# First phase of a conditioned transformer block: directions ahead of the rotations, both normalisations on ScalarE, gates inside the last group, masks loaded in the setup

## The chip, the cores and the metric

One core of a Trainium2 chip runs the whole program. The metric is the time of one execution on the device in microseconds, taken as the median of several runs.

## What is computed

Two batch elements of 2048 tokens with 256 channels go through a conditioned block: a layer norm that is scaled and shifted by vectors of a condition, an attention of 8 heads of 32 dimensions with a second "geometric" attention beside it, a gated residual, a second layer norm of the same kind, and two layers of local attention with a feed-forward part. The change lies in what leads to the first attention:

```python
mod = (_silu(L0_c) @ L0_wmod).reshape(L0_c.shape[0], 6, 1, -1)
sa, ca, ga, sb, cb, gb = ...                   # planes 0 to 5 of mod
ga = (2 * (ga >= 0) - 1) * jnp.maximum(jnp.abs(ga), 0.25)     # gb the same
h = _layernorm(x, axis=-1) * (1 + ca) + sa
# inside the attention, x is this h
xn = (x - mu) * jax.lax.rsqrt(var + 1e-05) * ln_g + ln_b
q, k, v = xn @ Wq.T, xn @ Wk.T, xn @ Wv.T      # in heads
q, k = _apply_rope(q, cos, sin), _apply_rope(k, cos, sin)
attn = softmax(where(causal, q @ k.T * scale, -inf))
qp, kp = einsum('bhtd,hd->bht', q[..., :3], head_dirs), ...   # the same of k
geo_attn = softmax(where(causal, qp[..., :, None] * kp[..., None, :], -inf))
```

A row's maximum of the geometric scores needs only the running maximum and minimum of kp up to that token. The kernel computes those as "directions".

## The kernel before

The program is a row of blocks, each with its own instruction stream per engine; at the end of a block the engines wait for each other. `setup_phase` computes the condition's six planes `S.mod` and the first normalisation of the first group. `qkv_phase`, here "the first phase", runs over 8 groups (`GROUPS`) of 512 tokens (four tiles of 128), four groups for each batch element. `attention_phase` then runs over 16 pairs of batch element and head, and the projection and the two layers follow. Each engine works its instructions in the order of the code and waits on semaphores; nothing is reordered.

Within a group n of the first phase, with lines of the kernel before:

- VectorE takes `statistics(n+1)` of the tokens in `xin` (mean and variance, `var` at L410). Then it makes four rotations (u = 0 to 3: two halves of q, two of k), each three instructions: `rot_c` L443, `rot_s` L444, their sum `qk` L449. A rotation waits for the product in `qk_ps`, which has two buffers, and releases it after L444. Between the rotations stand pieces of the next group: after u = 0 `modulated` (the normalised `xhat`, L418, times 1 + ca, L421), and behind it `directions(n-1)` (L462 to L469, on 8 partitions); after u = 1 `shifted` (`h_now`, L426, and its statistics, `var` at L429); after u = 2 `normed` (`hn`, L435). `low_part` (L453) subtracts the rounded part `hi` from `qk`. The group ends with two of these.
- GpSimd loads the tokens (L307) and raises the variance plus epsilon to the power -1/2: `rstd` at L309 for the first normalisation and at L302 for the second. The load for group n+2 is issued behind the second power of group n+1.
- ScalarE copies: `hi` (L328) after each rotation, `values` from `v_ps` (L331) after the third and fourth, the two rows of dots (L340), the transposed tokens `xnt` with the norm's gain and bias (L319), and `h_now` to its keeping place (L321).
- TensorE multiplies for the four rotations (L367), for the values (L377), makes the dots of q with the directions (L387), transposes `hn` of the next group (L356), and makes the dots of k (L387). The last waits for the copy of the dots of q, since both use one bank.
- SyncE sends a group's parts of q and k (eight stores, L279), then the directions' row of the group before (`send_geo`, L270), then the two rows of dots (L284, L285). The directions of a group wait until the row of the group before has landed, because they write the same tile `run`.

After the last group VectorE makes the `gates` (planes 2 and 5 of `S.mod`, L475 to L481) and the last directions, and SyncE sends their row as its last instruction of the phase.

In the attention's block GpSimd first issues three loads of masks (L913 to L915), which TensorE's first product (L971, L973) needs. SyncE loads the dots (L870), then the second head's operands (L516), then the geo rows (L788); TensorE transposes the dots (L1028) after three products. VectorE clears its tiles (L1151 to L1156) and takes chunk maxima (L1091).

## Time and profile before

| what | before |
|---|---|
| median of 3 runs | 2773.08 us (2772.15 to 2776.82) |
| profiled execution | 2774.7 us, span 2773.0 |
| TensorE / VectorE / ScalarE / GpSimd busy | 92% / 79% / 56% / 20% of the span |
| first phase, from VectorE's first instruction in its block to the first memset of the next | 23.00 to 263.25 us |
| attention's first product | 270.98 us |

The page's line of busy tenths gives a rough map; the first four of its forty slices are the setup and the first phase. The stretches, the timelines of single engines and the lines of single instructions give the rest. Times in a timeline are counted from the start of the span.

### The profile page before, as it was taken

To read this page: it belongs to the slowest core of one execution; us is meant where nothing else is said; L and a number is where in the kernel's file an instruction comes from. 1 tells how busy PE (TensorE), PEld (TensorE's weight loads), DVE (VectorE), ACT (ScalarE), POOL (GpSimd) and SP (SyncE) were. 2 spreads that over 40 slices of the span, in tenths; PEclk is the share of its full clock that TensorE was granted. 3 is DMA by queue.
4 is the path that set the end of the run, shared out by engine and by line. 5 is a ranking of instruction groups with operands and counts; after the bars stand their busy time and mean duration, and the time that the engine had idled before them with its cause. 6 is when DMAs were issued, how large, how long until landed. Compare 5 with 4: busy or idle time off the path is not lost. (4 is left out here: it accounts for less than half of the span.)

```text
span 2773.0 us, 45283 instructions
## 1 busy us (share of the span) xinstructions
PE 2563.4 (92%) x14104; PEld 1546.1 (56%) x14104; DVE 2187.4 (79%) x4633; ACT 1563.8 (56%) x3449; POOL 549.9 (20%) x389
## 2 busy tenths in 40 slices
PE   7886999999999999996999999989989999997998
PEld 3333433333333333334677777678867777775777
DVE  5877999999999999985788888656558888885665
ACT  1221566667766666762666666634336666664442
POOL 1100011111111100106333333200023333331000
PEclk9998899999999999998999999999989999999999
DMA  3234355445455445453100000030020000001121
GB/s 127 78 115 115 85 139 141 120 110 132 112 139 140 121 108 128 119 180 110 59 16 20 17 15 21 16 131 20 7 60 10 9 8 9 8 13 47 46 67 39
DMA packets 124741, 204.95 MB, mean 74 GB/s; under 512 B 22736, under 2 KB 71952, under 8 KB 121280
## 3 DMA queue, kind: packets, MB, share of 16 engines
q1 hardware_dynamic: 111856, 170.39, 22.1%
q0 software_dynamic: 8688, 21.27, 2.7%
q10 hardware_dynamic: 4080, 11.86, 1.2%
q8 instruction: 58, 0.95, 0.1%
q14 instruction: 59, 0.48, 0.1%
HBM read 125.44 MB, written 54.13 MB: 65 GB/s over the span
## 5 line engine op out<-in xcount | busy, mean ns | idle before, releaser
L1059 ACT ACTIVATE probs<-st_ps 128x512 f32<-128x512 f32 (+3 forms) x640 | 339.9, 531 | 294.1 <-PE st_ps L988 163.7
L1112 DVE SCALAR_TENSOR_TENSOR geo_x<-geo_rows,kp_t 128x512 f32<-128x512 f32 (+3 forms) x640 | 438.1, 708 | 4.5 <-ACT probs L1061 4.5
L1091 DVE TENSOR_REDUCE chunk_max<-a_ps 128x1 f32<-128x512 f32 (+3 forms) x640 | 359.1, 603 | 41.1 <-PE a_ps L971 27.0
L1061 ACT ACTIVATE probs<-geo_x 128x512 f32<-128x512 f32 (+3 forms) x640 | 361.4, 565 | 13.9 <-DVE geo_x L1118 13.8
L1391 PE MATMUL local_in_ps<-w_local,local_ht 128*128 128x512 f32 x1152 | 324.4, 419 | 9.5 <-ACT local_sq L1533 5.4
L1552 ACT ACTIVATE local_probs<-local_s_ps,local_bias,local_inv 128x256 f32<-128x256 f32 x512 | 283.2, 564 | 14.0 <-DVE local_bias L1647 14.0
L1830 PE MATMUL ff_ag_ps<-ff_ht_parts,w 128*128 128x512 f32 (+1 forms) x1056 | 257.6, 402 | 17.0 <-DVE ff_gate L1939 8.9
L1003 PE MATMUL o_ps<-probs,vx_first 128*33 128x512 f32 (+3 forms) x1280 | 270.6, 544 | 0.0
L1003 PE MATMUL o_ps<-probs,vx_ 128*33 128x512 f32 (+3 forms) x1280 | 270.3, 544 | 0.0
L1559 ACT ACTIVATE local_pt<-local_pt_ps 128x512 f32<-128x512 f32 x256 | 152.5, 596 | 207.7 <-PE local_pt_ps L1449 199.6
L1643 DVE TENSOR_REDUCE local_top<-local_s_ps 128x4 f32<-128x1024 f32 x128 | 156.8, 1225 | 121.2 <-PE local_s_ps L1435 121.2
L1391 PEld LDWEIGHTS local_in_ps<-w_local,local_ht 128*128 128x128 f32 x1152 | 209.1, 194 | 58.7 <-issue 18.8
L1830 PEld LDWEIGHTS ff_ag_ps<-ff_ht_parts,w 128*128 128x128 f32 (+1 forms) x1056 | 198.8, 191 | 71.0 <-DVE ff_gate L1939 16.6
L1654 DVE TENSOR_SCALAR local_probs<-local_probs,local_rden 128x256 f32<-128x256 f32 x512 | 223.0, 477 | 9.0
L1722 POOL TENSOR_TENSOR local_inv<-local_norm,half 128x16 f32<-128x16 f32 x64 | 186.5, 2915 | 175.3 <-DVE local_norm L1632 108.1
L1843 PE MATMUL ff_y_ps<-ff_w,ff_act_t 128*128 128x256 f32 x1152 | 148.6, 285 | 14.5 <-DVE ff_act_t L1945 13.9
L1459 PE MATMUL local_o_ps<-local_pt,local_v_ring 128*64 128x128 f32 x2048 | 154.6, 282 | 3.3 <-ACT local_pt L1559 3.1
L1449 PE MATMUL local_pt_ps<-ident,local_probs 128*128 128x128 f32 x1024 | 149.9, 279 | 6.5 <-DVE local_probs L1654 1.4
L367 PE MATMUL qk_ps<-xnt,w_qkv 128*128 128x512 f32 x256 | 128.2, 659 | 26.3 <-DVE rot_s L444 25.4
L1843 PEld LDWEIGHTS ff_y_ps<-ff_w,ff_act_t 128*128 128x128 f32 x1152 | 139.5, 190 | 21.2 <-DVE ff_act_t L1945 21.0
L971 PE MATMUL a_ps<-k_first,q_first 96*128 96x512 f32 (+2 forms) x320 | 120.8, 451 | 33.0 <-DMA later<-in_mask_t 16.9
L1435 PE MATMUL local_s_ps<-local_k_t,local_q_t 64*128 64x256 f32 x1024 | 146.1, 404 | 0.6 <-ACT local_q_t L1546 0.6
(193 smaller groups left out, 4155.0 us busy)
## 6 DMA issues: line engine op xcount, KB each, us to landing
geo_rows<-geo SPq DMA_DIRECT2D x64, 512.0 KB, 7.6
piece_lo<-in_pieces POOLq DMA_DIRECT2D x15, 768.0 KB, 5.7
weight_parts<-piece_hi SPq DMA_DIRECT2D x15, 768.0 KB, 3.4
weight_parts<-piece_lo SPq DMA_DIRECT2D x15, 768.0 KB, 6.0
raw<-out_t SPq DMA_DIRECT2D x128, 64.0 KB
shares_in<-shares SPq DMA_DIRECT2D x64, 128.0 KB, 4.7
q_first<-q_parts SPq DMA_DIRECT2D x24, 256.0 KB, 4.2
k_first<-k_parts SPq DMA_DIRECT2D x24, 256.0 KB, 6.3
```

Source lines behind the costliest of these rows:

```text
L1003: ins = pe.matmul(o_ps[kind * HALF:kind * HALF + VW, g % 2, off:GTOK], vx[s][:, j, :], probs[:, i % PSLOTS, kind, off:GTOK], start=j == 0, ...
L1059: act.activation(probs[:, s % PSLOTS, 0, off:GTOK], st_ps[:, (b * NB + s) % STBANKS, off:GTOK], ACT.Exp).then_inc(q["st_used"], 1)
L1061: act.activation(probs[:, s % PSLOTS, 1, off:GTOK], geo_x[:, s % GSLOTS, off:GTOK], ACT.Exp).then_inc(q["probs_ready"], 1)
L1091: dve.reduce_max(chunk_max[:, it, c:c + 1], a_ps[:, n % ABANKS, 0:width], AX.X).then_inc(q["a_used"], 1)
L1112: ins = dve.scalar_tensor_tensor(out[:, off:GTOK], geo[:, 1, at], kp_t[:, j, ds(b, 1)].rearrange("p o -> p o"), geo[:, 0, at], ALU.add, AL ...
L1391: last = pe.matmul(in_ps[:, j, :], ht[:, p, a, k, :], w[:, b, k, j * INNER:(j + 1) * INNER], start=i == 0, stop=i == len(steps) - 1)
L1552: last = act.activation(probs[:, hd, :], s_ps[:, a, x % 2 * 2 * P:(x % 2 + 1) * 2 * P], ACT.Exp, bias=bias[:, hd:hd + 1], scale=inv[:, p, ...
L1643: dve.tensor_reduce(top[:, hs].rearrange("p (x a) -> p x a", x=2), s_ps[:, :, :].rearrange("p a (x n) -> p x a n", x=2), AX.X, ALU.max).th ...
L1654: last = dve.tensor_scalar(probs[:, hd, :], probs[:, hd, :], rden[:, hd:hd + 1], None, ALU.mult)
L1722: pool.tensor_tensor(inv[:, p, :], norm2[:, :], S.half[:, :], ALU.pow).then_inc(q["inv_done"], 1)
L1830: last = pe.matmul(ag_ps[0:rows, x % 2, half, :], w1[:, a, k, c0:c0 + rows], ht_parts[:, b, k, :], start=i == 0, stop=i == len(steps) - 1)
L1843: last = pe.matmul(y_ps[:, t, :], act_t[:, a, x, t * P:(t + 1) * P], w2[:, b, x, :], start=(x, i) == (0, 0), stop=x == HC - 1 and i == len ...
```

## The change

Five things are changed.

1. `directions(n-1)` stands at the start of group n, behind `statistics(n+1)` and ahead of the first rotation. SyncE sends the row of group n-1 at the start of its turn n, ahead of the eight stores. The last row is sent as the first instruction of SyncE in the attention's block; the tiles for it lie on the other side of the memory.
2. Both normalisations go from VectorE to ScalarE, as `rstd * x + offset` with `offset = -mean * rstd`. VectorE makes the negated mean (`centre`), GpSimd multiplies. ScalarE does the first (`normalised`) at the start of a group and the second (`normed`) ahead of its fourth `hi`.
3. ScalarE keeps `h_now` (`keep`) at the end of its group and no longer between `xnt` and the second copy of dots.
4. `gates` is cut in two, for planes 2 and 5, and runs in the last group behind its first and second rotation; the addition on plane 4 stands ahead of the last `low_part`.
5. The three masks are loaded by GpSimd in the setup, into tiles that stay. Two tiles of the attention (`raw_0`, `raw_1`) change places in memory.

```diff
@@ Shared @@
+        self.mask_n, self.mask_t = sb("mask_n", [P, P], BF16), sb("mask_t", [P, P], BF16)
+        self.later = sb("later", [P, P])
@@ setup_phase, gpsimd @@
                 pool.dma_start(S.ident_bf[:, :], io["ident"]).then_inc(rounded, 16)
+                pool.dma_start(S.mask_n[:, :], io["mask_n"]).then_inc(S.attention_masks_in, 16)
+                pool.dma_start(S.mask_t[:, :], io["mask_t"]).then_inc(S.attention_masks_in, 16)
+                pool.dma_start(S.later[:, :], io["mask_t"]).then_inc(S.attention_masks_in, 16)
@@ new helper @@
+def send_geo(sp, S, n):
+
+    heads, tokens = group_place(n)
+    sp.wait_ge(S.first["geo_ready"], n + 1 + START)
+    sp.dma_start(S.geo[heads, 1, tokens], S.last_geo[:, :]).then_inc(S.first["geo_out"], 16)
@@ qkv_phase, sync @@
                 def send(n, geo_too):
+                    if geo_too:
+                        send_geo(sp, S, n - 1)
                     sp.wait_ge(q["hi_done"], 4 * n + 4 + START)
                     sp.wait_ge(q["lo_done"], 4 * n + 4 + START)
...
-                    if geo_too:
-                        send_geo(n - 1)
                     sp.wait_ge(q["dot_used"], 2 * n + 2 + START)
...
-                send_geo(GROUPS - 1)
@@ gpsimd @@
                 def second_scale(n):
                     pool.wait_ge(q["var2"], n + 1 + START)
                     pool.tensor_tensor(rstd[:, 1, :], var[:, 1, :], S.half[:, 0:GT], ALU.pow).then_inc(q["rstd2"], 1)
+                    pool.wait_ge(q["rstd2"], 2 * n + 1 + START)
+                    pool.tensor_tensor(offset[:, 1, :], centre[:, 1, :], rstd[:, 1, :], ALU.mult).then_inc(q["rstd2"], 1)
...
                     pool.tensor_tensor(rstd[:, 0, :], var[:, 0, :], S.half[:, 0:GT], ALU.pow).then_inc(q["rstd1"], 1)
+                    pool.wait_ge(q["rstd1"], 2 * n + 1 + START)
+                    pool.tensor_tensor(offset[:, 0, :], centre[:, 0, :], rstd[:, 0, :], ALU.mult).then_inc(q["rstd1"], 1)
@@ scalar @@
+                def keep(n):
                     act.activation(S.h1[:, ds(n * GT, GT), :], h_now[:, :, :], ACT.Copy).then_inc(q["h_kept"], 1)
 
+                def normalised(n):
+                    act.wait_ge(q["rstd1"], 2 * n + 2 + START)
+                    for t in range(GT):
+                        last = act.activation(xhat[:, t, :], xin[:, t, :], ACT.Identity, bias=offset[:, 0, t:t + 1], scale=rstd[:, 0, t:t + 1])
+                    last.then_inc(q["x_used"], 1)
+
+                def normed(n):
+                    act.wait_ge(q["rstd2"], 2 * n + 2 + START)
+                    act.wait_ge(q["xt_ready"], CC * n + START)
+                    for t in range(GT):
+                        last = act.activation(hn[:, t, :], h_now[:, t, :], ACT.Identity, bias=offset[:, 1, t:t + 1], scale=rstd[:, 1, t:t + 1])
+                    last.then_inc(q["hn_ready"], 1)
+
                 def group(n, more):
+                    if more:
+                        normalised(n + 1)
                     for u in range(4):
+                        if u == 3 and more:
+                            normed(n + 1)
                         act.wait_ge(q["rope_done"], 4 * n + u + 1 + START)
...
                         act.activation(dots_sb[:, u, :], dot_ps[:, :], ACT.Copy).then_inc(q["dot_used"], 1)
+                    if more:
+                        keep(n + 1)
@@ vector @@
+                    dve.tensor_scalar(centre[:, 0, :], mv[:, :, 0], -1.0, None, ALU.mult)
                     dve.tensor_scalar(var[:, 0, :], mv[:, :, 1], EPS, None, ALU.add).then_inc(q["var1"], 1)
...
-                        dve.wait_ge(q["rstd1"], n + 1 + START)
-                        for t in range(GT):
-                            last = dve.tensor_scalar(xhat[:, t, :], xin[:, t, :], mv[:, t, 0:1], rstd[:, 0, t:t + 1], ALU.subtract, ALU.mult)
-                        last.then_inc(q["x_used"], 1)
                         dve.wait_ge(q["x_used"], n + 1 + START)
...
                     if more:
                         statistics(n + 1)
-                    for u, piece in enumerate((modulated, shifted, normed, None)):
+                    if begun:
+                        directions(n - 1, first)
+                    for u, piece in enumerate((modulated, shifted, None, None)):
                         rotate(n, u)
                         if u:
                             low_part(n, u - 1)
                         if more and piece:
                             piece(n + 1)
-                        if u == 0 and begun:
-                            directions(n - 1, first)
+                        if not more and u in (0, 1):
+                            gates((2, 5)[u])
+                    if not more:
+                        dve.tensor_scalar(S.mod[:, 4, :, :], S.mod[:, 4, :, :], 1.0, None, ALU.add)
                     low_part(n, 3)
...
-                gates()
                 directions(GROUPS - 1, False)
@@ attention_phase @@
+            send_geo(sp, S, GROUPS - 1)
             sp.dma_start(dots[:, 1, :], S.dots).then_inc(q["dots_in"], 16)
...
-            pool.dma_start(mask_n[:, :], io["mask_n"]).then_inc(masks_in, 16)
-            pool.dma_start(mask_t[:, :], io["mask_t"]).then_inc(masks_in, 16)
-            pool.dma_start(later[:, :], io["mask_t"]).then_inc(masks_in, 16)
```

The rows below are the instructions of an engine in the order of the built program, with the shape of what each writes; x4 means four in a row. First VectorE at the start of group 1, before:

```order
L410 TENSOR_SCALAR var<-mv 128x4
L443 SCALAR_TENSOR_TENSOR rot_c<-qk_ps,cos_t 128x512
L444 SCALAR_TENSOR_TENSOR rot_s<-qk_ps,sin_t 128x512
L449 TENSOR_TENSOR qk<-rot_c,rot_s 128x512
L418 TENSOR_SCALAR xhat<-xin,mv,rstd 128x256 x4
L421 TENSOR_TENSOR xhat<-xhat,mod 128x1024
L462 SCALAR_TENSOR_TENSOR run<-dots_sb 8x512
L463 SCALAR_TENSOR_TENSOR run<-dots_sb 8x512
L465 COPY carry<-run 8x1 x2
L467 SCALAR_TENSOR_TENSOR run<-dots_sb,run 8x512
L468 SCALAR_TENSOR_TENSOR run<-dots_sb,run 8x512
L469 SCALAR_TENSOR_TENSOR run<-run 8x512
```

The same place in the changed program:

```order
L446 TENSOR_SCALAR centre<-mv 128x4
L447 TENSOR_SCALAR var<-mv 128x4
L488 SCALAR_TENSOR_TENSOR run<-dots_sb 8x512
L489 SCALAR_TENSOR_TENSOR run<-dots_sb 8x512
L491 COPY carry<-run 8x1 x2
L493 SCALAR_TENSOR_TENSOR run<-dots_sb,run 8x512
L494 SCALAR_TENSOR_TENSOR run<-dots_sb,run 8x512
L495 SCALAR_TENSOR_TENSOR run<-run 8x512
L469 SCALAR_TENSOR_TENSOR rot_c<-qk_ps,cos_t 128x512
L470 SCALAR_TENSOR_TENSOR rot_s<-qk_ps,sin_t 128x512
L475 TENSOR_TENSOR qk<-rot_c,rot_s 128x512
L454 TENSOR_TENSOR xhat<-xhat,mod 128x1024
```

The directions have moved ahead of the first rotation, the four instructions that normalise `xhat` are gone, and a `centre` has come in. Next ScalarE in its loop, from the values behind the third rotation to those behind the fourth; REGISTER_ALU and ISA are small instructions that set up the next wait or address. Before:

```order
L331 ACTIVATE values<-v_ps 128x512
L325 REGISTER_ALU
L328 ACTIVATE hi<-qk 128x512
L330 REGISTER_ALU
L331 ISA
L331 ACTIVATE values<-v_ps 128x512
```

and changed:

```order
L363 ACTIVATE values<-v_ps 128x512
L346 REGISTER_ALU
L348 ACTIVATE hn<-h_now,offset,rstd 128x256 x4
L357 REGISTER_ALU
L360 ACTIVATE hi<-qk 128x512
L362 REGISTER_ALU
L363 ISA
L363 ACTIVATE values<-v_ps 128x512
```

The four instructions for `hn` now stand in ScalarE's queue between the values of the third rotation and the `hi` of the fourth. Last GpSimd from the end of the first phase to the attention's first instructions, before:

```order
L260 UNCONDITIONAL_BRANCH
L901 UNCONDITIONAL_BRANCH
L913 DMA mask_n<-in_mask_n 128x128
L914 DMA mask_t<-in_mask_t 128x128
L915 DMA later<-in_mask_t 128x128
L946 MEMSET k_first 2x2048
```

and changed:

```order
L278 UNCONDITIONAL_BRANCH
L929 UNCONDITIONAL_BRANCH
L971 MEMSET k_first 2x2048
L971 MEMSET k_ 2x2048
L933 COPY vx_first<-values 128x16x32
```

The three loads have gone from here to the setup.

## Rows read from the trace of the kernel before

**Rows 1.** Stretches: us; busy (x instructions) of PE, PEld, DVE, ACT, POOL; PEclk, DMA, GB/s.

```profile
0.00:22.00 22.00, 12.46 (x24) 5.27 (x24) 5.63 (x21) 2.80 (x4) 2.05 (x7) 1.00 0.69 255
...
115.00:144.00 29.00, 24.16 (x66) 11.13 (x66) 23.29 (x53) 7.05 (x12) 2.78 (x3) 0.94 0.27 92
```

**Rows 2.** Timeline, VectorE, group 3: start us, us, what [idle before <-releaser].

```profile
120.75 0.69 DVE L443 SCALAR_TENSOR_TENSOR rot_c<-qk_ps,cos_t 128x512 f32<-128x512 f32 x1 [4.61 <-PE qk_ps L367]
...
122.78 1.38 DVE L418 TENSOR_SCALAR xhat<-xin,mv,rstd 128x256 f32<-128x256 f32 x4
...
125.86 1.27 DVE L462 TENSOR_TENSOR_SCAN run<-dots_sb,carry 8x512 f32<-8x512 f32 x1 [0.26 <-DVE xhat L421]
...
130.50 0.67 DVE L443 SCALAR_TENSOR_TENSOR rot_c<-qk_ps,cos_t 128x512 f32<-128x512 f32 x1
...
138.13 0.68 DVE L453 TENSOR_TENSOR lo<-qk,hi 128x512 fp32r<-128x512 f32 x1
...
149.48 0.69 DVE L443 SCALAR_TENSOR_TENSOR rot_c<-qk_ps,cos_t 128x512 f32<-128x512 f32 x1 [4.12 <-PE qk_ps L367]
```

**Rows 3.** Timeline, TensorE: ends of groups 0, 3 and 6, the slow product.

```profile
57.87 1.88 PE L387 MATMUL v_ps<-qk,dirs 128*8 128x512 f32 x4 [1.31 <-ACT values L331]
...
131.82 5.24 PE L367 MATMUL qk_ps<-xnt,w_qkv 128*128 128x512 f32 x8 [4.43 <-DVE rot_s L444]
...
143.75 1.88 PE L387 MATMUL v_ps<-qk,dirs 128*8 128x512 f32 x4 [0.41 <-issue]
145.56 4.99 PE L367 MATMUL qk_ps<-xnt,w_qkv 128*128 128x512 f32 x11
...
228.97 1.88 PE L387 MATMUL v_ps<-qk,dirs 128*8 128x512 f32 x4 [0.35 <-issue]
```

**Rows 4.** Timeline, ScalarE, end of group 3.

```profile
142.06 0.64 ACT L328 ACTIVATE hi<-qk 128x512 fp32r<-128x512 f32 x1 [2.55 <-DVE qk L449]
...
143.08 0.57 ACT L340 ACTIVATE dots_sb<-v_ps 8x512 f32<-8x512 f32 x1
...
144.88 1.04 ACT L321 ACTIVATE x<-h_now 128x1024 f32 x1
145.83 0.57 ACT L340 ACTIVATE dots_sb<-v_ps 8x512 f32<-8x512 f32 x1
```

**Rows 5.** Timeline, ScalarE, projection phase, and GpSimd's offset by line.

```profile
1257.34 2.09 ACT L578 ACTIVATE normed<-x,offset,rstd 128x256 f32<-128x256 f32 x4 [7.66 <-POOL offset L595]
...
L595 POOL TENSOR_TENSOR offset<-centre,rstd 128x4 f32<-128x4 f32 x8 | 1.6, 202 | 0.6
```

**Rows 6.** One line, the token load L307: time from issue to landing; its issue in group 3.

```profile
137.34 0.79 POOL L307 DMA_DIRECT2D xin<-in_x  x1
...
DMA to landing us min/median/max: 4.2/4.3/4.6
```

**Rows 7.** The line L657 and its longest instance: ns min/median/max, then timeline.

```profile
L657 DVE TENSOR_SCALAR centre<-mv x8: 170/170/986, 1245.8 to 1285.8; 128x4 f32<-128x4 f32 x8
...
1253.96 0.99 DVE L657 TENSOR_SCALAR centre<-mv 128x4 f32<-128x4 f32 x1
```

**Rows 8.** Timeline, end of the first phase: gates, geo row, last directions, next phase.

```profile
250.03 0.42 DVE L478 TENSOR_SCALAR sgn<-mod 128x512 f32<-128x512 f32 x1
...
254.37 0.60 SPq L270 DMA_DIRECT2D geo<-run  x1
...
257.60 1.27 DVE L462 TENSOR_TENSOR_SCAN run<-dots_sb,carry 8x512 f32<-8x512 f32 x1 [3.11 <-DMA geo<-run]
...
263.25 0.11 DVE L1151 MEMSET chunk_max<- 128x64 f32 x1 [0.94 <-PEq L260]
```

**Rows 9.** Timeline, start of the attention: load of the dots, first product, transposes.

```profile
263.16 0.32 SPq L870 DMA_DIRECT2D geo_rows<-dots  x1
...
270.98 0.48 PE L971 MATMUL a_ps<-k_first,q_first 96*128 96x128 f32 x1 [16.94 <-DMA later<-in_mask_t]
...
272.53 1.89 PE L1028 MATMUL st_ps<-ident,geo_rows 16*128 16x16 f32 x16
```

More of the change, by code:

```diff
@@ L244, in qkv_phase @@
         sgn, mag = sb("sgn", [P, B, C]), sb("mag", [P, B, C])
-        run = [sb(f"run{k}", [H, GTOK]) for k in range(2)]
-        carry = sb("carry", [H, 2])
+        dots_sb = sb("dots_sb", [H, 2, GTOK], side="right")
+        run = [sb(f"run{k}", [H, GTOK], side="right") for k in range(2)]
+        carry = sb("carry", [H, 2], side="right")
+        centre, offset = sb("centre", [P, 2, GT]), sb("offset1", [P, 2, GT])
+        S.last_geo = run[0]
         h_now = sb("h_now", [P, GT, C])
@@ L263, in _ @@
             def _(sp):
-                def place(n):
-                    return ds(n // GPB * H, H), ds(n % GPB * GTOK, GTOK)
-                def send_geo(n):
-                    heads, tokens = place(n)
-                    sp.wait_ge(q["geo_ready"], n + 1 + START)
-                    sp.dma_start(S.geo[heads, 1, tokens], run[0][:, :]).then_inc(q["geo_out"], 16)
                 def send(n, geo_too):
+                    if geo_too:
+                        send_geo(sp, S, n - 1)
                     sp.wait_ge(q["hi_done"], 4 * n + 4 + START)
@@ L428, in shifted @@
                     c.link(ln_stats(dve, c, stats, mv, carrier[:, :], lambda t: [h_now[:, t, :]]))
+                    dve.tensor_scalar(centre[:, 1, :], mv[:, :, 0], -1.0, None, ALU.mult)
                     dve.tensor_scalar(var[:, 1, :], mv[:, :, 1], EPS, None, ALU.add).then_inc(q["var2"], 1)
-                def normed(n):
-                    dve.wait_ge(q["rstd2"], n + 1 + START)
-                    dve.wait_ge(q["xt_ready"], CC * n + START)
-                    for t in range(GT):
-                        last = dve.tensor_scalar(hn[:, t, :], h_now[:, t, :],
-                                                 mv[:, t, 0:1], rstd[:, 1, t:t + 1], ALU.subtract, ALU.mult)
-                    last.then_inc(q["hn_ready"], 1)
                 def rotate(n, u):
@@ L683, in __init__ @@
         sb, _, _ = allocators(nc, ctx, ctx)
-        self.out_t = sb("out_t", [P, 2, GTOK], side="right")
-        self.raw = [sb(f"raw_{s}", [P, 2, GTOK], side="right") for s in range(2)]
+        raw_odd = sb("raw_1", [P, 2, GTOK], side="right")
         self.shares = sb("shares_in", [P, 2, GTOK], side="right")
         self.sums = sb("sums_in", [P, T * 2 // P], side="right")
+        self.out_t = sb("out_t", [P, 2, GTOK], side="right")
+        self.raw = [sb("raw_0", [P, 2, GTOK], side="right"), raw_odd]
         self.summed = sb("summed", [P, GTOK], side="right")
@@ L741, in attention_phase @@
     probs = sb("probs", [P, PSLOTS, 2, GTOK])
[L742 to L743 removed]
+    mask_n, mask_t, later = S.mask_n, S.mask_t, S.later
     share, out_t, raw, shares, sums, summed = ahead.share, ahead.out_t, ahead.raw, ahead.shares, ahead.sums, ahead.summed
```

31 lines of the change are left out of this document (15 added, 16 removed).

## Prediction

> **What bounds the kernel now.** The table of stretches says where to look. A group of 512 tokens in the first phase takes 29 us, and TensorE is busy for 24.2, VectorE for 23.3, ScalarE for 7.1 and GpSimd for 2.8 of it [rows 1]. Nobody is saturated, so the period is a loop of waits and I read it from the timelines of the engines. VectorE stands idle 4.61 us at a group's start, until TensorE has the first product of queries (L443) [rows 2]. TensorE in its turn starts the last product of the group 4.43 us late, because VectorE had not emptied the buffer: it was busy with 1.59 us of normalising xhat (L418) and 4.64 us of directions (L462 to L469) [rows 2, 3]. So two engines wait for each other once in a group. The loop begins at TensorE's last directions product of a group (L387), which I call S: 57.87 for group 0 and 228.97 for group 6, so six periods take 171.1 us, 28.52 each [rows 3].
>
> At S, ScalarE has just worked through a short queue: hi and values (1.02 us from 142.06), then the copy of the first dots, after which S starts at 143.75, 1.69 us behind hi [rows 3, 4].
>
> **The change, a steady group.** I walk once round the new loop from S.
> 1. TensorE's product ends and ScalarE copies it (L340). Before, the copy started 2.08 us after S, right behind the keeping copy of h (L321, ends 145.92); that now comes later, and the product itself (1.88) ends at 145.63, so I take 1.95 for its start. The copy takes 0.57, with a little for the signal 2.55 us from S to the first directions pass [rows 3, 4].
> 2. The directions now stand before the first rotation: 4.64 us [rows 2]. They need no product of this group, so they fill what was the wait. The product for the rotation is there at S+5.73 (before: S at 143.75, the wait at L443 over at 149.48 [rows 2, 3]), and the directions end at S+7.2, so VectorE no longer waits there.
> 3. From the first rotation to the end of the third VectorE took 120.75 to 138.13, 17.38 us [rows 2]. Away go the normalisation, 1.59, the directions, 4.64, and the pause of 0.26 ahead of them; a `centre` of about 0.08 comes in. That leaves 10.97.
> 4. ScalarE then does hi and values, 1.02, the four normalisations of hn, and the 1.69 to the next S. The four stand ahead of the last hi in its queue, and behind them the whole way to S waits. The same form runs in the later projection phase: four take 2.09 us, and the small `offset` on GpSimd 0.20 [rows 5]. Together 4.8. Its scale is ready early enough: a power takes 1.0 us on GpSimd (2.78 busy in a group, less 0.79 for the load's issue, halved [rows 1, 6]) and the offset 0.20, and both run while VectorE does the third rotation.
>
> The sum is 2.55 + 4.64 + 10.97 + 4.8 + 0.1 for signals = 23.05 us. I look at what else could be late. TensorE: its own work in a group is 24.2 us with eight matmuls at the slower clock; at the clock of the others (0.454 us each, 4.99 for 11) the eight cost 3.6 instead of 5.24 [rows 1, 3], so 22.5. That is close beneath. Token loads: GpSimd issues one right after the second scale, and it lands 4.2 to 4.6 us after that [rows 6]; before, the issue (137.34) came 6.84 us behind the second rotation's start (130.50), now that rotation starts at S+10.5 and a centre and an offset stand ahead of the issue, so S+17.9; plus 4.3 it is S+22.2, while VectorE asks for it at S+22.7. Hidden, by half a microsecond. ScalarE's first normalisation (another 2.09) starts at about S+3.5 and is asked for at S+9.2; hidden.
>
> Here a rule of the Trainium skill speaks against the move. "ScalarE: Activation LUTs" (Rules for kernel authors) sends adds and multiplies to VectorE and gives about 0.3 us plus 0.83 ns per element for an ACTIVATE. That is an estimate of 0.51 us for 256 elements and the trace agrees, with 0.52 (a quarter of 2.09) [rows 5]. The four steps cost more than on VectorE, 2.09 for its 1.29 to 1.59; if both engines stood on the path all the time the move would lose 0.7 us twice in a group. Only the second is on the path here.
>
> GpSimd's power of the first scale now runs beside the first pass of the directions. What that costs no group of before shows, since VectorE was idle then. The nearest row is in the projection phase: a `centre` that began while GpSimd added two tensors took 0.99 us, where the median of eight is 0.17 [rows 7]. Bounds: nothing, or 0.7 us (the time for which power and offset would still run when the pass wants to start). I take 0.3 since only part of the span overlaps: 23.4 us a group. "GPSIMD Engine Reference" (Specifications) says that GpSimd shares its SBUF interface with VectorE, with contention where VectorE has two SBUF inputs, as these passes have; by that rule alone it would be the 0.7, 2.4 us more in six groups.
>
> Six periods: 6 x (28.52 - 23.4) = **30.7 us saved**.
>
> **Start and group 0.** The normalisation of hn, four instructions of VectorE like those at L418 (1.38), becomes 2.09 on ScalarE behind an offset of 0.20, so everything begins 0.9 us later [rows 2, 5]. In group 0 TensorE runs through; its S waited 1.31 us for ScalarE [rows 3], and that wait goes, because VectorE is done some 2.7 us sooner. Together -0.2, which I count as 0. The three mask loads now stand in the setup, where TensorE waits for its first weights. They are 128 KB, half a microsecond at the 255 GB/s of the setup [rows 1]; between 0 and 0.5, and I take **0.3 lost**.
>
> **Last group and the boundary.** Before: from S of group 6 (228.97) to the first memset of the attention (263.25), 34.3 us [rows 3, 8]. In it the gates ran after the group's products, from 250.03 for 4.46 us, and the last directions then waited another 3.11 us until the geo row, which was queued behind eight stores, had landed [rows 8]. Now: directions end S+7.2; four rotations of 1.93 with two subtractions of 0.6 (8.9) and two gates of 2.23 between them make S+20.6; the last two subtractions and the 0.35 on plane 4 make S+22.2. The last directions run S+24.9 to S+29.5 (1.69 and 2.55 behind the last rotation, 4.64 long) and no longer wait for a transfer. SyncE sends eight stores (4.5) and two rows of dots from S+26.8, the last issued at S+27.4; a row like it landed 3.2 us after its issue (254.37 to 257.60) [rows 8], so the phase ends at about S+30.6 and the memset comes at S+31.1. **3.2 us saved.** The gates are not hidden where they stand; they cost the same 4.46 us ahead of the last products that they cost behind them before, and what is won is the wait.
>
> **Start of the attention.** TensorE's first product waited for the third mask until 270.98, 7.7 us after VectorE's first memset [rows 8, 9]. With masks in place it can run at once. The next thing late is the load of the dots, issued at 263.16 as SyncE's first; it now stands behind the last geo row (0.3). If it lands 3.2 us after its issue like the small row above, it is there at 266.65 on the clock of before; the transposes that need it (L1028) ran at 272.53 [rows 8, 9]. So 5.9 are saved and not 7.7. The loads that follow, for the second head and of the geo rows, then begin closer to each other and can crowd. Between 0 and 2 us; I take 0.6. **5.3 us saved.** Behind this the attention's engines follow each other, and I find no fixed point in it for which they would wait.
>
> **Sum:** 30.7 - 0.3 + 3.2 + 5.3 = **38.9 us**. The profiled execution took 2774.7 us (span 2773.0), so 2735.8; against the median of 2773.08, 1.6 lower, it is **2734.2 us**.
>
> **The rivals.**
> *The loop is longer than I walk it.* If the scans take the whole 0.7, ScalarE's four instructions do not overlap the wait for the third rotation, and the loop's register work adds to each step, a group takes 24.4: 6 us less saved, 2740. For it: the group from 120.75 to 149.48 took 28.73, 0.2 more than the mean [rows 2].
>
> *It is shorter,* 22.5, the bound by TensorE: 5.4 more, 2728.8. It needs ScalarE to be no part of the loop, against which its queue speaks.
>
> *The masks don't free the start.* Something else would hold TensorE's first product for the same time, such as the second head's load. Then 2739.5. The row names only the mask as what it waited for [rows 9].
>
> *The first phase gains, and the attention gives it back* by waiting for something set by the transfers, up to 30 us: 2745 to 2765. Nothing in the rows shows it.
>
> *Slower.* The token load gets onto the path. Directions could then start at the load's landing plus 2.3 us of statistics, and the period is 17.65 us plus the time to landing. With 4.3 that is 22, below the 23.4. It decides the period from 5.8 us on, and eats the whole gain (39 us, or 6.5 us a group) from 12.3 us to landing; at 15 the time is 2790. The seven landings of before lie within 4.2 to 4.6 [rows 6], and the stores that could crowd it still come behind it.
>
> *The change does not do what it says* in the clock: the product that ran slow after 4.43 us of waiting stays slow. TensorE's clock in that stretch was 0.94 of full on average [rows 1]; it would then be 24.2 a group, 2739. Its waits fall to about 1 us, so I count this with the longer loop.
>
> **How the numbers follow.** My forecast, with its own range of 2730 to 2738: 0.64. Longer loop 0.14, shorter 0.10, masks 0.06, gain given back 0.03, slower 0.03. The range 2727 to 2743 takes in the first four but for the ends of the shorter and longer loop. A difference of 0.2% (5.5 us) can be told from none: faster by more than that 0.96, same 0.01, slower 0.03.
>
> **What would show it.** The page of the changed kernel should show rotations' wait at the group's start gone; S to S at 23 to 24 us; the directions starting 2.5 us behind S with GpSimd's power beside them; normalisations of 0.52 us on ScalarE ending about when the fourth rotation does; VectorE's first memset of the attention near 229, its first chunk maximum within 3 us of that. Wrong would be a wait of VectorE for the token load, or a first product of the attention that still waits for a transfer.

## Result and the profile after

| | before | changed |
|---|---|---|
| median of 4 runs each, same chip | 2774.06 us (2772.15 to 2776.82) | 2732.91 us (2727.59 to 2735.83) |
| profiled execution, span | 2774.7, 2773.0 | 2730.8, 2729.1 |

The ratio is 0.985, 95% interval 0.983 to 0.9868: 41 us, or 1.5%, faster. The forecast was 2734.2 us.

A group first. The stretch of the changed kernel from 80 to 103 us (columns as in [rows 1]):

```profile
80.00:103.00 23.00, 22.23 (x64) 10.45 (x64) 21.05 (x47) 10.63 (x20) 3.81 (x5) 1.00 0.34 118
```

TensorE is now busy for 22.2 of 23 us and its clock is granted in full, where it had 24.2 of 29 at 0.94 [rows 1]. From S of group 0 to S of group 6 it takes 137.56 us, 22.93 a group, where it was 28.52 [rows 3]. Both ends, and two S in between, in TensorE's timeline (start, duration, what, idle before and its releaser):

```profile
57.45 1.88 PE L423 MATMUL v_ps<-qk,dirs 128*8 128x512 f32 x4
...
99.79 1.88 PE L423 MATMUL v_ps<-qk,dirs_q 128*8 128x512 f32 x4 [0.37 <-ACT values L363]
101.84 1.09 PE L392 MATMUL tp<-ident,hn 128*128 128x128 f32 x8 [0.17 <-ACT hn L348]
103.27 1.88 PE L423 MATMUL v_ps<-qk,dirs 128*8 128x512 f32 x4 [0.34 <-issue]
...
126.38 1.88 PE L423 MATMUL v_ps<-qk,dirs 128*8 128x512 f32 x4 [0.34 <-issue]
...
195.01 1.88 PE L423 MATMUL v_ps<-qk,dirs 128*8 128x512 f32 x4 [0.34 <-issue]
```

TensorE's only waits in a group are the three of 0.37, 0.17 and 0.34 us. The 4.43 us of waiting for `rot_s`, and the product at the slower clock behind it, are gone [rows 3].

VectorE from S (103.27) on:

```profile
105.90 1.27 DVE L488 TENSOR_TENSOR_SCAN run<-dots_sb,carry 8x512 f32<-8x512 f32 x1 [0.77 <-ACT dots_sb L372]
107.10 1.25 DVE L489 TENSOR_TENSOR_SCAN run<-dots_sb,carry 8x512 f32<-8x512 f32 x1
...
110.54 0.67 DVE L469 SCALAR_TENSOR_TENSOR rot_c<-qk_ps,cos_t 128x512 f32<-128x512 f32 x1
...
121.62 0.69 DVE L479 TENSOR_TENSOR lo<-qk,hi 128x512 fp32r<-128x512 f32 x1
...
125.36 0.69 DVE L479 TENSOR_TENSOR lo<-qk,hi 128x512 fp32r<-128x512 f32 x1 [0.54 <-ACT hi L360]
126.23 1.41 DVE L232 BATCH_NORM_STATS2 stats<-xin 128x6 f32<-128x256 f32 x4 [0.17 <-DMA xin<-in_x]
```

The first rotation (110.54) has no wait any more; it had 4.61 [rows 2]. ScalarE and GpSimd beside it:

```profile
105.22 1.03 POOL L320 TENSOR_TENSOR rstd<-var,half 128x4 f32<-128x4 f32 x1 [5.68 <-DVE var L447]
106.33 0.84 POOL L322 TENSOR_TENSOR offset<-centre,rstd 128x4 f32<-128x4 f32 x1
...
107.20 2.07 ACT L341 ACTIVATE xhat<-xin,offset,rstd 128x256 f32<-128x256 f32 x4 [0.49 <-POOL offset L322]
...
121.73 0.63 ACT L360 ACTIVATE hi<-qk 128x512 fp32r<-128x512 f32 x1 [5.16 <-DVE qk L475]
122.27 0.58 ACT L363 ACTIVATE values<-v_ps 128x512 f32 x1
122.75 2.06 ACT L348 ACTIVATE hn<-h_now,offset,rstd 128x256 f32<-128x256 f32 x4
124.71 0.62 ACT L360 ACTIVATE hi<-qk 128x512 fp32r<-128x512 f32 x1
```

The end of the phase and the start of the attention, VectorE, SyncE's queue and TensorE:

```profile
219.91 1.27 DVE L488 TENSOR_TENSOR_SCAN run<-dots_sb,carry 8x512 f32<-8x512 f32 x1 [2.71 <-ACT dots_sb L372]
...
222.43 0.60 SPq L295 DMA_DIRECT2D dots<-dots_sb  x1
...
225.68 0.11 DVE L1176 MEMSET chunk_max<- 128x64 f32 x1 [1.06 <-PEq L278]
225.79 0.44 PE L996 MATMUL a_ps<-k_first,q_first 96*128 96x128 f32 x1 [6.54 <-PEq L278]
...
228.88 1.88 PE L1053 MATMUL st_ps<-ident,geo_rows 16*128 16x16 f32 x16 [1.51 <-DMA geo_rows<-dots]
```

The first product runs as soon as the block begins, no longer 7.7 us later, and the transposes follow the memset by 3.20 us instead of 9.28 [rows 8, 9].

Where 43.65 us went, up to VectorE's first `geo_x` of the attention (288.75 us before, 245.10 now):

| stretch | before | changed | saved | forecast |
|---|---|---|---|---|
| start to S of group 0 | 57.87 | 57.45 | 0.42 | -0.3 |
| six groups | 171.10 | 137.56 | 33.54 | 30.7 |
| S of group 6 to the memset | 34.28 | 30.67 | 3.61 | 3.2 |
| memset to first `geo_x` | 25.50 | 19.42 | 6.08 | 5.3 |

From the first `geo_x` to the end of the span both take the same, 2484.25 and 2484.00 us. In executions of the changed kernel that part varies, from 2480.4 to 2484.2 in three of them, and over all kernels here from 2477.0 to 2490.0, with no code changed in it. So medians tell a microsecond or two badly, and below the marks of the profiled executions decide. One of the four executions of e1 below took 5096.46 us, nearly twice the others, and nothing on record says why; it is left out of e1's median.

### The profile page after: what moved, and what is told of

Its sections match the earlier page's. It is cut to its first block and busy times, and to the rows that moved or that the text cites. A ratio compares the mean times of both kernels' runs of the same rounds, so it can differ in the third digit from the quotient of the medians.

```text
span 2729.1 us, 45326 instructions
## 1 busy us (share of the span) xinstructions
PE 2551.3 (93%) x14104; PEld 1541.0 (56%) x14104; DVE 2171.9 (80%) x4588; ACT 1589.6 (58%) x3509; POOL 554.8 (20%) x404
## 3 DMA queue, kind: packets, MB, share of 16 engines
q1 hardware_dynamic: 111856, 170.39, 22.2%
## 5 line engine op out<-in xcount | busy, mean ns | idle before, releaser
L1742 POOL TENSOR_TENSOR local_qk_nat<-local_rot_c,local_rot_s 128x512 f32<-128x512 f32 x64 | 82.8, 1294 | 303.4 <-PE local_pt_ps L1438 302.2
L1475 PEld LDWEIGHTS local_pt_ps<-ident,local_probs 128*128 128x128 f32 x1024 | 113.9, 141 | 51.3 <-issue 23.0
```

What stands on the lines that cost most here:

```text
L1475: last = pe.transpose(pt_ps[:, x % 2, (2 * a + s) * P:(2 * a + s + 1) * P], probs[:, 2 * x + a, s * P:(s + 1) * P], S.ident[:, :])
```

## The experiments

All on the changed kernel unless it is said otherwise, with the kernel before run beside each. "Period" is the mean of six from S to S. Ratios are to the kernel before.

| run | period | S6 to memset | memset to transposes | first `geo_x` | median, ratio [interval] |
|---|---|---|---|---|---|
| before | 28.52 | 34.28 | 9.28 | 288.75 | |
| changed | 22.93 | 30.67 | 3.20 | 245.10 | 2732.91, 0.985 |
| a0 | 22.93 | 30.63 | 3.28 | 245.22 | 2732.36, 0.9849 [0.9831, 0.9867] |
| a1 | 22.93 | 30.64 | 3.45 | 246.22 | 2731.48, 0.9835 [0.9821, 0.9849] |
| e1 masks late | 22.93 | 30.71 | 9.42 | 250.08 | 2734.72, 0.985 [0.9828, 0.9872] |
| e2 gates last | 22.93 | 29.46 | 3.17 | 243.18 | 2727.95, 0.9834 [0.9815, 0.9853] |
| e3 directions back | 26.34 | 34.67 | 3.26 | 269.62 | 2760.51, 0.9945 [0.9927, 0.9963] |
| e4 directions alone | 25.37 | 30.03 | 9.18 | 264.94 | 2751.78, 0.9915 [0.989, 0.994] |
| e5 hn on VectorE | 23.87 | 30.70 | 3.39 | 250.54 | 2738.34, 0.9864 [0.9839, 0.9889] |
| e8 keep ahead | 23.87 | 30.73 | 3.27 | 250.64 | 2740.05, 0.9875 [0.9856, 0.9894] |
| e9 one tile on VectorE | 22.90 | 30.70 | 3.09 | 243.85 | 2732.42, 0.9849 [0.9824, 0.9873] |
| e10 gates and dots | 22.92 | 29.46 | 3.12 | 243.10 | 2725.55, 0.9825 [0.9808, 0.9842] |
| e11 fewer products | 22.92 | 30.61 | 3.14 | 244.46 | 2730.72, 0.9832 [0.9811, 0.9853] |
| e12 half scale | 22.39 | 30.77 | 3.39 | 241.02 | 2727.09, 0.9819 [0.9801, 0.9836] |

**The changed kernel again**, twice.

> The changed kernel itself, on this chip, as the reference for the others: about 41 us below the kernel before (2733), S to S (from one group's last directions product to the next) 22.9 us, from S of group 6 to VectorE's first memset of the attention 30.7 us, from that memset to the transposes of the dots 3.2 us.

> The changed kernel once more, on the same chip as the three others, so that the smaller differences have their own reference. Period 22.93, S of group 6 to the first memset 30.6, memset to transposes 3.2, first geo_x at 245.1; median 2729 to 2736.

The period and the stretch from S of group 6 to the memset repeat within 0.05 us, and the stretch from the memset to the transposes within 0.25. The start does not: S of group 0 came at 57.45, 57.55 and 58.38.

**The directions' place.** e4 does this part alone, on the kernel before (only the last row stays in the first phase, where it was):

```diff
                 def send(n, geo_too):
+                    if geo_too:
+                        send_geo(n - 1)
...
-                    if geo_too:
-                        send_geo(n - 1)
...
+                    if begun:
+                        directions(n - 1, first)
                     for u, piece in enumerate((modulated, shifted, normed, None)):
...
-                        if u == 0 and begun:
-                            directions(n - 1, first)
```

> Kernel before with one part of the change: directions at the group's start and their row sent ahead of the eight stores. Normalisations stay on VectorE, gates and masks stay where they were. S to S = 2.65 + 4.64 + 16.3 + 1.7 = 25.3 us instead of 28.5, so 19 us in six periods, and 2 to 3 us at the last directions, which no longer wait for the row: 22 us faster than before. Rival: the wait for the first product just moves elsewhere (VectorE is 23 of 28.5 us busy and the normalisations keep it the bound): under 8 us.

and e3 puts them back behind the first rotation in the changed kernel, with SyncE's early row kept:

```diff
-                    if begun:
-                        directions(n - 1, first)
...
+                        if u == 0 and begun:
+                            directions(n - 1, first)
```

> Changed kernel with the directions back behind the first rotation and the product with 1 + ca; all else as changed. If the directions filled VectorE's wait for the first product, the wait comes back and the 4.64 us come on top: S to S = 5.7 + 10.9 + 4.6 + 4.8 = 26.1 us instead of 22.9, the run 19 to 22 us slower than the changed kernel. Rival: the gain was the normalisations', and the place of the directions is indifferent: under 5 us.

Alone the move is worth 3.15 us a group, and 23.8 us at the first `geo_x`. At the boundary it saves 4.25 us (30.03 for 34.28), more than the 3.61 of the whole change; the runs on the gates below say why. Undone it costs 3.41 a group. The wait it was meant to fill is back in e3, VectorE at the first rotation:

```profile
115.53 0.69 DVE L469 SCALAR_TENSOR_TENSOR rot_c<-qk_ps,cos_t 128x512 f32<-128x512 f32 x1 [4.18 <-PE qk_ps L403]
```

So more than half of the 5.59 a group is the order of VectorE's work. The rest comes with the two normalisations and the place of `keep`; the first normalisation was not moved back in any run. First `geo_x` of e3 comes 24.5 us later than in the changed kernel, more than the 19 to 22 expected of the run: 20.5 are the six groups (26.34 for 22.93), and 4.0 are lost at the boundary, where the last group has its directions on the path in the same way.

**The normalisation of hn on ScalarE, and what stands in its queue.** e5 gives hn back to VectorE as before:

```diff
-                        if u == 3 and more:
-                            normed(n + 1)
...
-                    for u, piece in enumerate((modulated, shifted, None, None)):
+                    for u, piece in enumerate((modulated, shifted, normed, None)):
```

> Changed kernel with the second normalisation (hn) back on VectorE, the first still on ScalarE. If VectorE's and ScalarE's parts of the loop follow each other, VectorE gets 1.29 us more ahead of the fourth rotation, ScalarE's 2.07 before the fourth hi go, and the 0.6 of the fourth subtraction's wait too: S to S = 2.55 + 4.64 + 10.97 + 0.6 + 1.29 + 1.93 + 1.7 = 23.7 us, 4 to 5 us slower than the changed kernel. Start of group 0 0.9 us earlier. Rival, by the plain cost of the two engines (2.07 against 1.38): the run is faster, by up to 4 us.

e8 leaves it on ScalarE and puts `keep` ahead of the last `hi`:

```diff
                         if u == 3 and more:
                             normed(n + 1)
+                            keep(n + 1)
...
-                    if more:
-                        keep(n + 1)
```

> Changed kernel with the keeping copy of h (1.04 us on ScalarE, 0.95 with its overlap) moved between the normalisation of hn and the fourth hi. If ScalarE's queue there is part of the loop, a group gets 0.95 us longer (23.9) and the run 5.7 us slower. Rival: TensorE is the bound (22.0 busy plus 0.9 of waits in 22.9) and ScalarE has slack; then a group gets at most 0.5 us longer.

Both cost 0.94 us a group, where 0.8 and 0.95 were expected. For e8 that is the keeping copy nearly in full, which ScalarE now does on the way to S; TensorE's row shows the wait (the line number differs by one):

```profile
104.89 1.88 PE L422 MATMUL v_ps<-qk,dirs 128*8 128x512 f32 x4 [1.28 <-ACT values L364]
```

1.28 where the changed kernel has 0.34. What stands ahead of the last `hi` in ScalarE's queue is on the path, and what stands behind it is free. For e5, ScalarE's four instructions take 2.06 and VectorE's 1.48 for the same work, and the move to the slower engine still gains, since they no longer delay the fourth rotation. A rival that prices the move by the two durations alone has the wrong sign. "ScalarE: Activation LUTs" (Rules for kernel authors) in the Trainium skill gives such multiplies to VectorE; its price for one agreed with the row, but the queues decided, not the price.

**Who bounds the new loop?** With TensorE at 22.2 of 23 us I had two readings: TensorE itself, or the ring through VectorE's rotations and ScalarE's queue. e9 was the first try, one of hn's four tiles back on VectorE, between the third rotation and the fourth:

```diff
-                    for t in range(GT):
+                    for t in range(GT - 1):
                         last = act.activation(hn[:, t, :], h_now[:, t, :], ACT.Identity, ...)
...
-                    for u, piece in enumerate((modulated, shifted, None, None)):
+                    for u, piece in enumerate((modulated, shifted, last_tile, None)):
```

> Changed kernel with one of the four tiles of hn normalised by VectorE, between the third and the fourth rotation, the other three by ScalarE. If ScalarE's queue is what the fourth hi waits for by about 0.5 us, a group gets 0.2 to 0.35 us shorter and the run 1 to 2 us faster than the changed kernel. Rival: TensorE is the bound; then no difference in S to S (below 0.1).

No gain (22.90): my theory missed it, and the rival, a bound by TensorE, seemed to hold. But e9's own trace speaks for the ring:

```profile
100.56 0.63 ACT L360 ACTIVATE hi<-qk 128x512 fp32r<-128x512 f32 x1 [0.37 <-DVE qk L482]
...
102.24 1.88 PE L423 MATMUL v_ps<-qk,dirs 128*8 128x512 f32 x4 [0.56 <-ACT values L363]
```

ScalarE saves 0.49 us (1.57 for 2.06), but its last `hi` now waits 0.37 for VectorE's fourth rotation, which comes 0.43 later, counted from S (19.38 for 18.95). TensorE then waits 0.56 ahead of S, where it was 0.34. The work had only changed hands within the ring. To be sure, each side was shortened on its own. e11 takes work from TensorE. It leaves two of the eight products of the values out, so it computes something else and only its time is used:

```diff
-                            for k in range(CC):
+                            for k in range(t, CC):
                                 last = pe.matmul(v_ps[:, u, t * C:(t + 1) * C], ...,
-                                                 start=k == 0, stop=k == CC - 1)
+                                                 start=k == t, stop=k == CC - 1)
```

> The changed kernel with two of the eight products of the values left out in each group (for half the tokens only one half of the channels is summed), 0.9 us less of TensorE's work in each group. Theory A, TensorE bounds the period (22.2 of 22.93 busy): the period falls by 0.9 to 22.0. Theory B, the loop through VectorE's rotations and ScalarE's queue bounds it, and TensorE only follows closely: the product of the dots waits for ScalarE's copy of the values (0.37 in the changed kernel) and will wait 0.9 longer, some 1.3 us, and the period stays at 22.9 (22.85 to 22.95). After the run in which a tile of hn was moved to VectorE without a gain I hold B for likelier, 0.7.

and e12 takes work from VectorE, by leaving half of `xhat` unscaled:

```diff
-                    c.link(dve.tensor_tensor(xhat[:, :, :], xhat[:, :, :], mod(n, 1), ALU.mult))
+                    part = xhat[:, 0:GT // 2, :]
+                    c.link(dve.tensor_tensor(part, part, ..., ALU.mult))
```

> The changed kernel with VectorE multiplying only two of the four tiles of xhat by 1 + ca, 0.61 us less of VectorE's work between the first and the second rotation; the other two tiles stay unscaled. Theory B (the loop through VectorE): everything from the second rotation on comes 0.6 sooner, until TensorE stops it: its busy time is 22.07 to 22.2 and it has a gap of 0.34 ahead of the last product, so the period falls to 22.4 (22.3 to 22.5). Theory A (TensorE bounds): the period stays at 22.9, and VectorE waits 0.6 more.

The stretch from 80 to 103 us and TensorE's product of the dots in e11, then in e12:

```profile
80.00:103.00 23.00, 21.26 (x61) 9.69 (x60) 20.89 (x47) 10.64 (x20) 3.78 (x5) 1.00 0.35 118
...
99.30 1.88 PE L423 MATMUL v_ps<-qk,dirs_q 128*8 128x512 f32 x4 [1.23 <-ACT values L363]
```

```profile
80.00:103.00 23.00, 22.60 (x66) 10.59 (x66) 20.93 (x52) 10.76 (x20) 3.78 (x5) 1.00 0.37 124
...
97.69 1.88 PE L423 MATMUL v_ps<-qk,dirs_q 128*8 128x512 f32 x4
```

e11 has 0.9 us less of TensorE's work in a group and the same period to 0.01; the work turns into a longer wait for ScalarE's copy, 1.23 for 0.37. e12 has 0.54 us less on VectorE (0.68 where it was 1.22), and the period falls by the same 0.54. The ring through VectorE and ScalarE bounds the loop and TensorE follows closely: in e12 its waits for `values` and `hn` are gone, and only the 0.34 ahead of the last product is left. Those two waits, 0.37 and 0.17, are the 0.54 that the period fell by. So at 22.39 the group is TensorE's own work and that 0.34; whether anything more could be gained from VectorE was not tried.

**The masks.** e1 moves the three loads back to the attention's block:

```diff
-                pool.dma_start(S.mask_n[:, :], io["mask_n"]).then_inc(S.attention_masks_in, 16)
...
+            pool.dma_start(S.mask_n[:, :], io["mask_n"]).then_inc(S.attention_masks_in, 16)
```

> Changed kernel with the three mask loads back in the attention's block. If the masks held the attention's first product and nothing else would, the first product comes about 5 us after VectorE's first memset again (in the kernel before 7.7), the transposes behind it, and the run is 5 to 6 us slower than the changed kernel; the setup gives back 0.3. Rival: the second head's load or the dots' load hold the start anyway; then the difference is under 1 us.

TensorE's first product in e1, the wait it replaces in the changed kernel:

```profile
232.31 0.47 PE L996 MATMUL a_ps<-k_first,q_first 96*128 96x128 f32 x1 [14.34 <-DMA later<-in_mask_t]
```

It comes 7.9 us behind the memset (about 5 were expected), the transposes 9.42, and first `geo_x` 6.2 later counted from the memset. As the forecast had it, the masks were worth about 6 and not 7.7, since the load of the dots comes next. By the median e1 is only 2.4 us above a0 on the same chip, where 5 to 6 were expected; its first `geo_x` comes 4.9 us later than a0's (6.2, less 1.4 by which its S of group 0 came earlier), and the other 2.5 lie within the spread of the part behind. What the loads cost in the setup can't be told: S of group 0 came at 56.18 without them, and at 56.3 to 58.4 in eleven executions with them.

**The gates.** e2 puts both behind the last group's products, where they stood before:

```diff
-                        if not more and u in (0, 1):
-                            gates((2, 5)[u])
...
+                        gates(2)
+                        gates(5)
```

> Changed kernel with the two gates and the addition on plane 4 behind the last subtraction of the last group. Theory A (my walk of the last group: VectorE sets its end, each gate costs its 2.23 us): the last directions start 3 to 4.5 us earlier and the run is 3 us faster. Theory B (in the last group TensorE's chain of products ends last: 14 us of products from 196.8, values 3.6, dots 1.8, ScalarE's copy, dots 1.8): the gates stand in shadow, the last directions start only 0.6 us earlier, and the run is 0.5 to 1 us faster.

VectorE in e2, from the end of the gates to the first memset of the attention:

```profile
217.76 0.69 DVE L506 SCALAR_TENSOR_TENSOR mod<-sgn,mag 128x512 f32<-128x512 f32 x1
218.72 1.27 DVE L488 TENSOR_TENSOR_SCAN run<-dots_sb,carry 8x512 f32<-8x512 f32 x1 [0.27 <-ACT dots_sb L372]
...
223.80 0.11 DVE L1176 MEMSET chunk_max<- 128x64 f32 x1 [0.37 <-PEq L278]
```

This is the expectation's theory B. Behind the products the gates fill the wait for the last dots: 0.27 is left of the 2.71 that the changed kernel has. The scan starts 0.52 sooner, counted from S of group 6 (24.38 for 24.90), and the memset another 0.7 sooner, since its wait falls from 1.06 to 0.37. Ahead of the last products the gates hold up the last `lo`, with it the eight stores and the row of dots behind them (issued at 222.43 in the changed kernel, 219.00 in e2). The memset follows that issue by 3.25 us in the changed kernel, 3.29 in e1 and 3.27 in e9, and by 4.80 in e2. From this I take it that in the first three the row's landing ends the phase, and in e2 VectorE does; the view itself names only TensorE's branch. So this part of the change is a loss, of 1.2 us, and not neutral.

**The best of them.** e10 is e2 with one thing more, the load of the dots ahead of the last geo row:

```diff
-            send_geo(sp, S, GROUPS - 1)
             sp.dma_start(dots[:, 1, :], S.dots).then_inc(q["dots_in"], 16)
+            send_geo(sp, S, GROUPS - 1)
```

> The changed kernel with both gates behind the last group's products, as in the run that put the gates last, and with the load of the dots issued ahead of the last geo row. Nobody needs the geo row before the geo rows are loaded, while the transposes wait for the dots. Theory: the gates give 1.2 us between the last S and the first memset, as they did alone (30.63 to 29.46), and the transposes follow the memset by 3.2 - 0.3 = 2.9 us, since an issue takes about 0.3 on SyncE's queue. First geo_x 1.5 to 2.3 us earlier than in the changed kernel (245.1 to 245.2): 243.2 at the latest. Rival: the geo row then lands later and the load of the geo rows behind it waits for it, and the transposes gain 0.3 that first geo_x doesn't show. Median near 2729, where the changed kernel has 2732.

```profile
223.69 0.32 SPq L897 DMA_DIRECT2D geo_rows<-dots  x1
...
223.78 0.11 DVE L1176 MEMSET chunk_max<- 128x64 f32 x1 [0.37 <-PEq L278]
...
226.90 1.88 PE L1053 MATMUL st_ps<-ident,geo_rows 16*128 16x16 f32 x16 [1.42 <-DMA geo_rows<-dots]
```

The load leaves 0.35 us earlier and takes 3.21 to be used, where it took 2.93 in e2 (224.04 to 226.97), so only 0.05 of the 0.3 arrives; that expectation missed. From S of group 6 to first `geo_x` e10 takes 48.8 us, and the changed kernel 50.1 and 50.3. Its median on the same chip, 2725.55, is the lowest of all and 5.9 below a1's, but the intervals overlap, and by the marks only 1.3 to 1.5 of that are its own, nearly all of it e2's (48.84).

## Why the prediction was right, and where it was off

**The walk, step by step**, from S of group 2 (103.27) to the next. Step 1, S to the first directions pass: 2.63 measured, 2.55 forecast. Step 2, the directions: 4.64, as forecast. Step 3, first rotation to the end of the third: 110.54 to 121.62, 11.08 for 10.97. Step 4, to the next S: 4.76 for 4.8 and 0.1 of signals. Together 23.11, where the sum without contention was 23.05. The four rows of hn take 2.06, its scale and offset are in time, and the rest of ScalarE's queue is as walked.

**The contention term was wrong.** I added 0.3 us a group for GpSimd's power beside the first pass. The pass takes 1.27 us, as in [rows 2], and the power 1.03. What is stretched is GpSimd's own `offset`: 0.20 alone, and 0.84 beside the first scan. It ends when that scan ends (106.33 + 0.84 and 105.90 + 1.27 are both 107.17), and so it is, within 0.01 us, in all six groups that have a scan there. The power, which already runs when the scan begins, keeps its 1.03 and doesn't hold the scan up. The seven instances in the changed kernel, and in e3, where the scans come later (ns min/median/max, then the places):

```profile
L322 POOL TENSOR_TENSOR offset<-centre,rstd x7: 198/757/996, 37.7 to 175.3; 128x4 f32<-128x4 f32 x7
```

```profile
L322 POOL TENSOR_TENSOR offset<-centre,rstd x7: 201/201/203, 37.7 to 192.3; 128x4 f32<-128x4 f32 x7
```

ScalarE's normalisation of xhat then starts 0.4 late (S+3.93), ends at 109.27, and is asked for at 112.55, so nothing comes of it. "GPSIMD Engine Reference" (Specifications) in the Trainium skill names contention where VectorE has two SBUF inputs. There is some, but its price fell on GpSimd and not on VectorE, and the estimate of 0.7 from that rule was too high.

**The mean is not the looped group.** I walked a group in the middle. The six periods of the changed kernel are 22.71, 23.11, 23.11, 23.10, 22.71 and 22.82. The three long ones are groups 2 to 4, which are VectorE's loop; the others are written out. The mean lies 0.18 below the looped group. With the 0.3 above this makes the gap from 23.4 to 22.93 but for roundings: six times 0.47 are 2.8 of the 4.75 us that the sum fell short.

**The rest of the shortfall.** Start and group 0: 0.42 saved instead of 0.3 lost. The setup's end moved by 0.31 in this pair (VectorE's first copy of `mod`: 21.00 for 20.69), and group 0 took 0.7 less than I gave it. That the first matches the forecast is luck: the same copy came at 20.34 to 21.83 in eleven executions with the loads there, and at 20.13, 20.33 and 20.69 in three without. S of group 0 varies by 2 us, so this term is not proved either way. The wait of 1.31 us ahead of S of group 0 did go, as forecast. Boundary: 3.61 for 3.2, with the row of dots issued at S+27.42 (forecast S+27.4) and the memset at S+30.67 (S+31.1). Start of the attention: 6.08 for 5.3; the transposes came 3.20 behind the memset, as the landing of the small row told, and of the 0.6 for crowding nothing was seen.

**The gates** were the step that was wrong in its reason. The prediction held that they cost their 4.46 us at either place and that the gain was the wait for the geo row. The gain is that wait, but at the old place the gates would now cost about nothing (e2), because VectorE waits there for TensorE and ScalarE in any case: behind both gates 0.27 us of that wait are still left.

**The rivals.** The token load stayed off the path, but not out of VectorE's waits. It landed in 4.2 to 4.4 us, as forecast, but behind S of group 2 it was issued at S+18.58 (121.85) and not at S+17.9, and VectorE waited 0.17 us for it at 126.23; behind those statistics it waits 0.68 for the dots anyway, so nothing is lost. In group 0 it waited much longer, and had another 4.46 us to wait for TensorE's first product behind it:

```profile
34.41 1.41 DVE L232 BATCH_NORM_STATS2 stats<-xin 128x6 f32<-128x256 f32 x4 [6.42 <-DMA xin<-in_x]
```

So a wait for the token load, named as a sign of being wrong, did appear, and was harmless. The longer loop did not come; the shorter one (22.5, bound by TensorE) is where e12 arrives, with 22.39. The clock is 1.00 in the loop, and the slow product is gone with the wait ahead of it. In e3 both are back; in e4 there is a shorter wait and no slow product:

```profile
125.01 5.40 PE L403 MATMUL qk_ps<-xnt,w_qkv 128*128 128x512 f32 x8 [2.83 <-DVE rot_s L470]
```

```profile
121.70 3.70 PE L367 MATMUL qk_ps<-xnt,w_qkv 128*128 128x512 f32 x8 [1.27 <-DVE rot_s L444]
```

The granted clock of that group was 0.94 in e3 and 1.00 in e4.

One sign named ahead was missed: the first chunk maximum was to come within 3 us of the attention's first memset, and came 3.61 behind it (229.29), right at the end of the long copy described in the last section.

The saving at the marks was 43.65 us against 38.9. That the time came within 1.3 us of the forecast owes something to the part behind, whose spread of several microseconds is larger than the miss: the profiled execution of the changed kernel lies 2.1 below its median.

## What to carry to other kernels

When two engines wait for each other once a period, move work that needs neither of them into the wait first: that alone gave 3.15 of 5.59 us. Then price a move between engines by what stands behind it in both queues up to the next hand-over, not by the two durations; here a copy of 1.04 us cost nothing behind the hand-over, and 0.94 ahead of it. A busy share of 97% doesn't prove a bound: shorten each candidate by itself and see which one the period follows.

## What was not expected of the hardware

GpSimd's `offset` on 128x4 took 0.76 us in the median and 1.00 at most beside VectorE's scans on 8 partitions, for 0.20 away from them, while the scans kept their 1.27 and 1.25. The length has no value of its own: it is what is left of the first scan when `offset` is asked for.

The other way round, two small instructions of VectorE grew while GpSimd cleared rows of k. VectorE and GpSimd in the changed kernel at the start of the attention, and the same two of VectorE before:

```profile
225.60 1.80 POOL L971 MEMSET k_first<- 2x2048 f32 x1 [35.82 <-POOLq L278]
...
226.89 0.53 DVE L1180 TENSOR_SCALAR share<-scales 64x8 f32<-64x8 f32 x1
227.44 1.84 DVE L1181 COPY share<-scales 64x8 f32<-64x8 f32 x1
227.46 1.80 POOL L971 MEMSET k_<- 2x2048 f32 x1
```

```profile
264.46 0.15 DVE L1155 TENSOR_SCALAR share<-scales 64x8 f32<-64x8 f32 x1
264.63 0.17 DVE L1156 COPY share<-scales 64x8 f32<-64x8 f32 x1
```

Before, the memsets stood behind the mask loads and began only at 265.35. The copy grew from 0.17 to 1.84 us, and each of the two ends with the memset beside it: 227.42 and 227.40, then 229.28 and 229.26. e1, made for another question, is a test of it. There the loads stand ahead of the memsets again, and the two are short again:

```profile
225.66 0.15 DVE L1180 TENSOR_SCALAR share<-scales 64x8 f32<-64x8 f32 x1
225.83 0.17 DVE L1181 COPY share<-scales 64x8 f32<-64x8 f32 x1
...
226.56 1.80 POOL L971 MEMSET k_first<- 2x2048 f32 x1
```

Since e1 moves the loads as well, it is not a test of the memsets alone. In the changed kernel the first chunk maximum starts only when the copy ends, but three maxima later VectorE waits 1.28 us for TensorE, so it costs nothing.

A group in VectorE's loop takes 0.29 us longer than a written-out one (group 2 beside group 6). That the loop is the cause was not tried. The difference arises in three steps of 0.1: ahead of the first scan, ahead of the first rotation's sum, and ahead of the second rotation.
